# Feed-forward stage of a two-layer decoder block: scaling and rounding of the second half moved into TensorE and PSUM, one ScalarE copy for two banks, half of the first bias on VectorE

## The reference, cut to what matters

```
def act_quant(x):
    scale = 127.0 / jnp.clip(jnp.max(jnp.abs(x), axis=-1, keepdims=True), 1e-05)
    q = jnp.clip(jnp.round(x * scale), -128.0, 127.0) / scale
def bitlinear158(x, w, b):
    xq = act_quant(rms_norm(x))
    wq = weight_quant(w)              # weights to -1, 0, 1 times a scale
    return jnp.einsum('bsd,od->bso', xq, wq) + b
# feed-forward: h = silu(bitlinear158(layernorm(x), w1, b1))      256 -> 1024
#               h = gelu(h); h = layer_norm(h, ln_g, ln_b)
#               x = x + bitlinear158(h, w2, b2)                  1024 -> 256
```

## Time and profile before

| what | us |
|---|---|
| median of 3 runs | 770.2 (769.21 to 771.85) |
| the profiled execution's own time | 765.48 |
| its span in the profile | 763.6 |

### The profile page before, as it was taken

How to read it: one execution, slowest core, us unless ns; L and a number is a source line. 1 busy time by engine, 2 the same in 40 slices (tenths; PEclk the granted TensorE clock), 3 DMA queues, 4 the chain that set the end, 5 groups by cost and what they waited for, 6 DMA issues and landing times. The chain is left out here.

```text
span 763.6 us, 15646 instructions
## 1 busy us (share of the span) xinstructions
PE 634.6 (83%) x4418; PEld 453.0 (59%) x4419; DVE 544.2 (71%) x1180; ACT 385.6 (50%) x829; POOL 329.3 (43%) x642
## 2 busy tenths in 40 slices
PE   4999999969999799798998678999997489715665
PEld 3788888854444375476776567877786333314444
DVE  4789888856999865333223788999995556379995
ACT  2677777750000033143331456777775256679993
POOL 1223222254767333611113453333332478468883
PEclk9999999999999879989999889999998599956666
DMA  8904100001322000274531130000000000000011
GB/s 302 412 7 134 57 0 0 1 1 27 53 46 52 14 1 20 105 228 132 158 103 55 41 126 2 3 1 0 0 1 1 0 1 0 0 1 0 5 50 55
DMA packets 27337, 41.93 MB, mean 55 GB/s; under 512 B 3520, under 2 KB 22608, under 8 KB 26400
## 3 DMA queue, kind: packets, MB, share of 16 engines
q1 hardware_dynamic: 23808, 31.14, 13.4%
q0 software_dynamic: 3488, 10.28, 3.8%
HBM read 31.15 MB, written 10.26 MB: 54 GB/s over the span
## 5 line engine op out<-in xcount | busy, mean ns | idle before, releaser
L216 POOL TENSOR_TENSOR var_eps<-mv,powers 128x1 f32<-128x1 f32 x96 | 19.8, 206 | 229.5 <-DVE mv L211 229.2
L450 ACT COPY wide<-ps 128x512 f32<-128x512 f32 x128 | 75.2, 587 | 37.6 <-PE ps L307 37.2
L523 DVE TENSOR_REDUCE work<-ps 128x8 f32<-128x1024 f32 x64 | 78.0, 1219 | 15.0 <-PE ps L299 14.9
L676 PE MATMUL ps<-ctxT,small 128*128 128x512 f32 x192 | 83.7, 595 | 1.1 <-ACT xnT_all L652 0.8
L307 PE MATMUL ps<-ident,work 128*128 128x128 f32 x512 | 80.1, 279 | 3.5 <-ACT wide L450 3.5
L526 DVE TENSOR_TENSOR work<-ps,work 128x1024 f32<-128x1024 f32 x64 | 78.4, 1225 | 5.3 <-DVE work L523 0.2
L445 ACT ACTIVATE work<-work 128x1024 f32<-128x1024 f32 x64 | 67.8, 1059 | 15.1 <-DVE work L526 14.6
L715 POOL TENSOR_TENSOR ctxT<-xn_all 128x1024 f32 (+1 forms) x32 | 60.0, 1895 | 24.1 <-PE ps L676 24.1
L307 PEld LDWEIGHTS ps<-ident,work 128*128 128x128 f32 x512 | 59.0, 142 | 15.8 <-issue 11.3
L676 PEld LDWEIGHTS ps<-ctxT,small 128*128 128x128 f32 x192 | 36.2, 191 | 46.6 <-issue 43.3
L219 POOL TENSOR_TENSOR rstd<-var_eps,powers 128x1 f32<-128x1 f32 x96 | 55.3, 576 | 7.5
(11 more groups left out here) (190 smaller groups left out, 1531.4 us busy)
## 6 DMA issues: line engine op xcount, KB each, us to landing
wide<-in_expert_gu SPq DMA_DIRECT2D x1, 4096.0 KB, 21.3
small<-hank SPq DMA_DIRECT2D x32, 128.0 KB, 3.7
sorted_x<-small POOLq DMA_DIRECT2D x1, 2944.0 KB, 11.9
work<-sorted_x SPq DMA_DIRECT2D x23, 128.0 KB, 2.1
sorted_y<-work POOLq DMA_DIRECT2D x23, 128.0 KB, 2.4
xn_all<-in_ctx_rev_t SPq DMA_DIRECT2D x1, 2048.0 KB, 10.9
wide<-in_expert_d SPq DMA_DIRECT2D x1, 2048.0 KB, 25.6
xn_all<-in_ffn_w SPq DMA_DIRECT2D x2, 1024.0 KB, 6.9
```

The lines of the kernel that those rows point to most:

```text
L450: act.copy(probT[r], T).then_inc(s["pT"], 1)
L523: dve.tensor_reduce(m, S2[g], AX.X, ALU.max).then_inc(s["mx"], 1)
L676: mm = pe.matmul(ps[4 * u + o], toep[u][:, c, lt * P:(lt + 1) * P], kv[u][:, c, half * 512:(half + 1) * 512], start=(c == 1 - lt), stop=(c ...
```

## The change

In the first half the bias b1 of the upper 512 columns no longer goes through PE. PE does one bias matmul (lower 512 columns), and the upper bank starts with the weight matmul. DVE computes from that bank, at the end of its body, `H = PSUM * unscale + b1` (new semaphore `h_bias`), and ACT's second Silu reads that from SBUF in place. `dve_first` runs two more bodies for it. The add of the output bias to x leaves POOL's body: it is now four operations on four tiles each (128x1024), two before the first mean of the second half and two after the first rstd.

In the second half LayerNorm's second step writes to the buffer q32 and not back to H, and the 128x1024 scaling on DVE is gone, with POOL's `factor`. DVE makes a diagonal of 128x128 from the identity times reciprocal times rms127, and PE multiplies the eight blocks with it as float32 matmuls (turn and scale in one), then adds the rounding constant with two bf16 matmuls of one row of ones against one row of the constant, 512 columns each. ACT copies both banks at once (1024 columns). Two small placeholder operations go (L1605, L1650). ACT does the Gelu of tile 1 ahead of the variance of tile 0.

```diff
                 if there(t - 2):
                     act.wait_ge(s["h_ps"], 2 * (t - 1))
                     act.wait_ge(s["factor"], 3 * (t - 1))
                     ...
-                    for j in range(2):
-                        act.activation(H[:, ds((t - 2) * INNER + j * 512, 512)], HB[u][j],
-                                       ACT.Silu, scale=unscale[u]).then_inc(s["silu"], 1)
+                    act.activation(H[:, ds((t - 2) * INNER, 512)], HB[u][0],
+                                   ACT.Silu, scale=unscale[u]).then_inc(s["silu"], 1)
+                    upper = H[:, ds((t - 2) * INNER + 512, 512)]
+                    act.wait_ge(s["h_bias"], t - 1)
+                    act.activation(upper, upper, ACT.Silu).then_inc(s["silu"], 1)
...
-                    for j in range(2):
-                        pe.matmul(HB[1 - u][j], diag[1 - u], b1[:, j * 512:(j + 1) * 512],
-                                  start=True, stop=False)
+                    pe.matmul(HB[1 - u][0], diag[1 - u], b1[:, 0:512], start=True, stop=False)
...
+                if there(t - 2):
+                    dve.wait_ge(s["h_ps"], 2 * (t - 1))
+                    dve.wait_ge(s["factor"], 3 * (t - 1))
+                    dve.scalar_tensor_tensor(H[:, ds((t - 2) * INNER + 512, 512)], HB[u][1], unscale[u],
+                                             b1[:, 512:1024], ALU.mult, ALU.add
+                                             ).then_inc(s["h_bias"], 1)
...
-                    pool.wait_ge(f.xn, f.base + t + 1)
-                    pool.tensor_tensor(tile_of(x, t), tile_of(x, t), row_bias[:, 2 * D:3 * D],
-                                       ALU.add).then_inc(s["x_bias"], 1)
+            def pool_x_bias(pool, first):
+                tiles = x[:, first * D:(first + 4) * D].rearrange("p (t d) -> p t d", d=D)
+                bias2 = row_bias[:, 2 * D:3 * D].unsqueeze(1).broadcast_to([P, 4, D])
+                pool.tensor_tensor(tiles, tiles, bias2, ALU.add).then_inc(s["x_bias"], 4)
+            TB2 = [psum[:, (4 + 2 * u) * 512:(6 + 2 * u) * 512] for u in range(2)]
+            Y = [ps[0], ps[1]]
...
+                act.activation(qT[u], TB2[u], ACT.Identity, bias=c_nmagic).then_inc(s["qT"], 1)
...
                 if there(t - 1):
-                    pe.wait_ge(s["rounded"], NB + t)
-                    wait(pe, s["qT"], NB + 2 * (t - 2))
+                    pe.wait_ge(s["ln"], t)
+                    pe.wait_ge(s["diag"], NB + t)
+                    wait(pe, s["qT"], NB + t - 2)
                     for c in range(8):
-                        mm = pe.transpose(TB2[1 - u][c // 4][:, c % 4 * P:(c % 4 + 1) * P],
-                                          q32[1 - u][:, c * P:(c + 1) * P], ident)
+                        pe.matmul(TB2[1 - u][:, c * P:(c + 1) * P], q32[1 - u][:, c * P:(c + 1) * P],
+                                  diag[1 - u], start=(c % 4 == 0), stop=False, skip_group_check=True)
+                    for k in range(2):
+                        mm = pe.matmul(TB2[1 - u][:, k * 512:(k + 1) * 512], ones_bf[0:1, :], magic[0:1, :],
+                                       start=False, stop=True, skip_group_check=True)
                     mm.then_inc(s["qT_ps"], 1)
...
-                    dve.scalar_tensor_tensor(Ht(t), Ht(t), rstd2[u], ln_b, ALU.mult, ALU.add
+                    dve.wait_ge(s["qT_ps"], NB + t - 1)
+                    wait(dve, s["squares"], NB + t - 1)
+                    wait(dve, s["abs"], NB + t - 1)
+                    dve.scalar_tensor_tensor(q32[u], Ht(t), rstd2[u], ln_b, ALU.mult, ALU.add
...
                     dve_inverse(dve, t - 1, 1 - u, 1)
+                    dve.wait_ge(s["inverse"], NB + t)
+                    dve.wait_ge(s["rms127"], NB + t)
+                    wait(dve, s["qT_ps"], NB + t - 2)
+                    dve.tensor_scalar(diag[1 - u], ident, inverse[1 - u], rms127[1 - u], ALU.mult, ALU.mult
+                                      ).then_inc(s["diag"], 1)
...
-                if there(t - 1):
-                    dve.wait_ge(s["factor"], made(1, t - 1) + 1)
-                    wait(dve, s["qT_ps"], NB + t - 2)
-                    dve.tensor_scalar(q32[1 - u], Ht(t - 1), factor[1 - u], MAGIC, ALU.mult,
-                                      ALU.add).then_inc(s["rounded"], 1)
...
             def gpsimd(pool):
...
                 pool.wait_ge(f.xn, f.base + NB)
+                pool_x_bias(pool, 0)
+                pool_x_bias(pool, 4)
                 pool_mean(pool, 0, 0)
+                pool_mean(pool, 1, 1)
                 pool_rstd(pool, 0, 0)
-                pool_mean(pool, 1, 1)
+                pool_x_bias(pool, 8)
+                pool_x_bias(pool, 12)
                 pipeline(pool, lambda t, u, i: pool_second(pool, t, u, i), 2, 1)
```

More of the change, by code:

```diff
@@ L1348, in feed_forward @@
                 "factor", "rounded", "diag", "qT_ps", "qT", "h_ps", "silu", "gelu", "mean",
-                "var", "eps2", "rstd", "centred", "ln", "y_ps", "x_bias", "x_new")}
+                "var", "eps2", "rstd", "centred", "ln", "y_ps", "x_bias", "x_new", "h_bias")}
             w32 = [xn_all[:, 0:2048], xn_all[:, 2048:4096]]
@@ L1409, in dve_weights @@
                     dve.memset(ones, 1.0).then_inc(s["ones"], 1)
+                    dve.memset(magic, MAGIC).then_inc(s["ones"], 1)
                 if t == 2:
@@ L1427, in made @@
             def made(k, t):
-                return 3 * t if k == 0 else 3 * NB + 2 * t
+                return 3 * t if k == 0 else 3 * NB + t
             def pool_rms(pool, t, u, k):
@@ L1440, in pool_rms @@
                 pool.wait_ge(s["rms"], n + 1)
-                wait(pool, s["factor"], made(k, t - 1))
+                wait(pool, s["factor"], made(0, t - 1 if k == 0 else NB))
+                if k == 1:
+                    pool.wait_ge(s["diag"], n - 1)
                 pool.tensor_tensor(rms127[u], rms[u], c_127, ALU.mult).then_inc(s["rms127"], 1)
@@ L1455, in dve_inverse, with pool_factors @@
                 dve.wait_ge(s["largest"], n + 1)
+                if k == 1:
+                    dve.wait_ge(s["diag"], n - 1)
                 dve.reciprocal(inverse[u], largest[u]).then_inc(s["inverse"], 1)
[L1458 to L1463, removed]
+            def pool_factors(pool, t, u):
+                pool.wait_ge(s["inverse"], t + 1)
+                pool.wait_ge(s["rms127"], t + 1)
+                wait(pool, s["rounded"], t - 1)
                 pool.tensor_tensor(factor[u], inverse[u], rms127[u], ALU.mult).then_inc(s["factor"], 1)
[L1465 to L1468, removed]
+                wait(pool, s["diag"], t - 1)
+                pool.tensor_tensor(inv_unscale[u], inverse[u], inv_wk[:, 0:1], ALU.mult
+                                   ).then_inc(s["factor"], 1)
             def pool_unscale(pool, t, u, k, read):
+                pool.wait_ge(s["largest"], NB * k + t + 1)
                 wait(pool, *read)
@@ L1523, in pe_first @@
                             mm = pe.matmul(HB[1 - u][j], qT[1 - u][:, c * P:(c + 1) * P],
-                                           wq[0][:, c, j * 512:(j + 1) * 512], start=False,
-                                           stop=(c == KT - 1))
+                                           wq[0][:, c, j * 512:(j + 1) * 512],
+                                           start=(j == 1 and c == 0), stop=(c == KT - 1))
                         mm.then_inc(s["h_ps"], 1)
@@ L1578, in act_var, with act_int @@
                                accum_out=var[u]).then_inc(s["var"], 1)
-            def act_int(act, t, u, half):
-                act.activation(qT[u][:, half * 512:(half + 1) * 512], TB2[u][half], ACT.Identity,
-                               bias=c_nmagic).then_inc(s["qT"], 1)
+            def act_int(act, t, u):
+                act.activation(qT[u], TB2[u], ACT.Identity, bias=c_nmagic).then_inc(s["qT"], 1)
             def act_second(act, t, u, i):
@@ L1604, in act_second @@
                     wait(act, s["var"], min(t + 2, NB) if isinstance(t, int) else t + 2)
-                    act.copy(tick_act, c_eps)
-                    act.activation(junk, Ht(t), ACT.Square, scale=INNER ** -0.5, accum_out=ms[u]
+                    act.activation(junk, q32[u], ACT.Square, scale=INNER ** -0.5, accum_out=ms[u]
                                    ).then_inc(s["squares"], 1)
@@ L1649, in dve_second @@
                     dve.wait_ge(s["largest"], NB + t - 1)
-                    dve.memset(tick, 0.0)
-                    dve.tensor_reduce(absmax[u], Ht(t), AX.X, ALU.max, apply_absolute_value=True
+                    dve.tensor_reduce(absmax[u], q32[u], AX.X, ALU.max, apply_absolute_value=True
                                       ).then_inc(s["abs"], 1)
-                if there(t - 1):
-                    dve.wait_ge(s["factor"], made(1, t - 1) + 1)
-                    wait(dve, s["qT_ps"], NB + t - 2)
-                    dve.tensor_scalar(q32[1 - u], Ht(t - 1), factor[1 - u], MAGIC, ALU.mult,
```

(3 more changed lines are left out.)

15 lines of the change are left out of this document (6 added, 9 removed).

## The result

The changed kernel takes 773.01 us, median of 20 runs (768.28 to 776.21), beside 770.2 of the kernel before: ratio 1.0035, 95% interval 1.002 to 1.005. It is slower by 2.8 us. The forecast was 766.7, faster; the range of 760.5 to 779 holds the time, the direction is wrong.

A forecast was written before the change was run, and what follows sets the result against it. A chain through POOL bounds the first half; DVE, with ACT close behind, the second. First half -6.3 plus second half +2.8 gave -3.5 us, 770.2 to 766.7; the 8-in-10 range was 760.5 to 779.

The forecast's parts named there:

- (a): First half: POOL's add leaves the body, 0.25 us a body, -3.2 us for 13 bodies.
- (c): First half: PE loses one of two bias matmuls; nothing in steady state, -1.5 us at the start, -1.6 at the end.
- (b): First half: DVE's new 128x512 operation reading PSUM takes 0.75 us and hides in DVE's idle time; charged 0.
- (d) to (f): Second half: DVE's body 4.6 us; ACT's single copy 1.21; PE's turn plus constant 2.55, loop 4.75 at 2.4 GHz.
- (g): Second half, PE's clock: first two steps 7.5 and 5.8 us, then 2.4 GHz; 15 steps 75.1 against 74.91, +0.2.
- rival A: Second half: PE's clock falls back, 2.8 us per slow step; 772 to 778 with two to four; chance 0.25.
- (h): Start of second half: POOL's two long adds delay the second rstd, +1.1 us; about +4 if they hold DVE.
- (i): Tail after the last transposes: serial, 2.55 for 1.04 us, +1.5 us; at 1.2 GHz up to +4.
- B: No change: step 4.95 us, or DVE's new operation does not hide, or long adds hold DVE; 769 to 770; chance 0.22.
- C: More gain: clock rises within first float32 matmuls, loop 4.6 us, (a) gives 0.35 a body; about 760.5; chance 0.13.

The follow-up runs named there:

- e12_adds_only: Kernel before with only POOL's output-bias add taken out of the first-half body, adds placed late, new start order, both bias matmuls kept on PE; 770.64 us, 1.0001.
- e4_fill: Changed kernel plus five unread bf16 matmuls of 512 columns behind each second-half turn; 761.4 us, 0.9966 of the kernel before.
- e2_second: Only the second half of the change; bias matmuls and POOL's adds in the first-half body as in the kernel before; 767.79 us, 1.0058.
- e9_swap_inplace: Changed kernel with PE's turn before weight matmuls, DVE's new x and POOL's unscale later, LayerNorm writing H in place, placeholders back; 764.93 us, 0.9936.
- e8_before_fill: Kernel before plus five unread bf16 matmuls of 512 columns behind each second-half turn; 763.12 us, 0.9976.
- e6_late: e4_fill with the long adds of tiles 8 to 11 and 12 to 15 moved behind POOL's bodies of tiles 1 and 2; 756.2 us, 0.9885.
- e7_warm: e6_late plus 14 unread matmuls of 512 columns before the first turn; 754.65 us, 0.9879.
- e3_swap: Changed kernel with PE's second-half body exchanged: turn of tile t-1 first, then weight matmuls of tile t-2; 811.01 us, 1.0621.

## Why the prediction was wrong

**(a) to (c), the first half: right in sum, with the shares wrong.** -6.3 forecast, -6.30 found. On the same tiles, the start brought -1.34 (forecast -1.5), the bodies -3.80 (-3.2), the end -1.16 (-1.6). (b) DVE's operation is 0.74 (forecast 0.75) and hides. But (c) said PE "is not the chain" in steady state. With the add gone and PE as before (e12_adds_only) the bodies gain only 2.0: PE, busy 9.34 of 10 us there, is the next limit, and nearly half of the bodies' gain is the bias matmul's. So (a) at -3.2 was too much for the add alone, and the 1.8 that (c) put at nothing made it up: that the sum fits is in part luck.

**(d) to (f), the prices: right.** Diagonal 0.35 (0.28 plus a wait was taken), copy 1.11 (1.21), turn 2.05 plus the constant, which ends 2.58 after the turn's start (2.55). A step at 2.4 GHz averages 4.81 over nine steps (4.75).

**(g), the clock: the step that failed.** The text took "2.4 GHz for the rest" after two steps, from one stretch of 4 us. Against its 75.1, the 15 steps took 81.66, 6.6 more: the first step +0.1, the second +0.9, three falls back +5.1 (1.75, 1.67 and 1.67), nine steps at full clock +0.5. e4_fill shows the cause: with PE's gaps filled the falls are gone, and the 15 steps are 5.6 shorter. The rows for it stood there: PE was moving between its levels in the second of the earlier trace rows, and the gaps of 1.4 us ahead of the weight matmuls were to stay., 2.73 busy of 4 us, have about the busy share that was forecast, but that did not settle it: in after PE is busy 7.17 of 10 us in the window at 1.00 just ahead of the one at 0.83.

The text weighed a rule of the Trainium skill, TensorE: Matmul & The Clock Gate, section "Part 4: PE-mode transpose", that transposes don't count as busy for the clock, and that by it rival A falls away. The turns of after are ordinary matmuls and the clock fell all the same, so that conclusion is refuted; the rule itself no run here tests.

**Rival A was the outcome,** with the right mechanism and the wrong price: 2.8 us a slow step. Two of the three falls cost 1.67, as they lasted for part of a step; the third, over two steps, 1.75. +5.1 was enough to eat the 3.5. Its 772 to 778 for two to four slow steps holds the 773.01.

**(h), the start: right in sum, from two wrong terms.** +1.1 forecast, +1.06 found. The new order at the start gained 2.0 (15.88 to 13.84 in e12_adds_only) and the new body another 1.4 (12.48 in e2_second), where the text took 1; the long adds cost 4.5, where it took 2.1. What it left out of the sum is what happened: beside an add DVE's 1.28 us became 3.36. The Trainium skill, SBUF — State Buffer, section "SBUF: two separate sides", has GpSimd and a VectorE operation with two SBUF inputs exclude each other for a whole instruction. The trace agrees: 3.36 is 1.28 and 2.08 of the 2.36 that one add takes alone. By the rule the text had the whole start at about +4; the adds did cost 4.5, and a gain that it had too small paid for it.

**(i), the tail: right.** +1.22 for +1.5, with the turn at 2.4 GHz.

**Rivals B and C.** B's long adds held DVE as it said, its common step of 4.95 did not come. C did not come: the first turn took 3.75 us and the second 3.62, both at 1.2 GHz.

Two things the text did not see. The change made DVE depend on the turn twice over, through q32, so that a slow PE stopped DVE as well (e9_swap_inplace: opened, 15 steps take 71.54). And the slow clock of before cost little because no such loop was the longest one: kept away, it gives the 15 steps 2.1 us there (e8_before_fill) and 5.6 in the changed kernel (e4_fill).

What stays open: which pattern of gaps makes the clock fall in step 7 and not in step 6, whose records look alike. Each kernel was profiled once, so how many falls another execution has is not known either.

## What to carry to other kernels

Before work is moved onto an engine whose clock moves between two levels, write the loop at both levels and ask what hides the slow one; if nothing does, either open the loop (in place, another order, one tile more of distance) or keep the engine busy with work that nobody reads. Put a long operation beside an engine that it holds up only where another engine is the limit, and look again when that limit is gone: the adds that were free in e6_late were not in e7_warm. When PE's body is swapped, look at what waits for its last part: e3_swap lost 6% to one wait of DVE that had been free.

## What the runs showed of the hardware that was not expected

- Work without use can be worth time: five bf16 matmuls of 512 columns in each step raised PE's busy time from 7.2 to 9.53 of 10 us, removed the falls of the clock and took 5.3 us off the stage.
- A POOL add of 128x1024 (2.34 to 2.36 us) makes DVE's 1.28 us LayerNorm step last 3.3 to 3.5 where both start together, whether it writes to H or to q32.
- ACT copies 1024 columns over two PSUM banks in 1.11 us, where two copies of 512 take 1.26 together.
